# First-layer weight rows loaded by groups of 32 partitions, and two small products moved ahead of the router's product

## The reference

```python
nx = layer_norm(x) * gamma + beta
q, k, v = nx @ Wq, ctx @ Wk, ctx @ Wv
weights = softmax(q k^T / 16)                    # over the 64 prototypes
evidence = weights @ v
combined = concat([nx, evidence, anchor])        # anchor: one row of 256 per batch
probs = softmax(combined @ router_W + router_b)  # 3 experts
h = silu(combined @ e_w1[e] + e_b1[e])           # 768 -> 512, per expert
routed = sum_e probs[e] * (h @ e_w2[e] + e_b2[e])
g = sigmoid(silu(combined @ gate_w1 + gate_b1) @ gate_w2 + gate_b2)
out = x + g * (routed @ out_w + out_b)
```

## Time and profile before

| what | value |
|---|---|
| median of 3 runs | 459.05 us (458.45 to 460.62) |
| the profiled execution | 458.27 us, span of its instructions 456.5 us |
| PE busy | 444.9 us (97%), 2070 matmuls |
| DVE / ACT / POOL busy | 269.5 (59%) / 246.4 (54%) / 93.8 us (21%) |
| mean granted PE clock | 0.987 |
| DMA queue of SP | 48.33 MB |
| the chain that ended last | PE 87%, DVE 3%, DMA 3%, ACT 3%, issue 2% |

### The profile page before, as it was taken

The page is one execution under the profiler, slowest core; times in us unless marked ns, Lnnn a source line. Parts: engine busy times, 40 slices in busy tenths (PEclk is TensorE's granted clock), DMA queues, the critical chain, the costliest instruction groups (busy, mean ns, idle before and its releaser), DMA issues.

```text
span 456.5 us, 6005 instructions
## 1 busy us (share of the span) xinstructions
PE 444.9 (97%) x2070; PEld 363.2 (80%) x2070; DVE 269.5 (59%) x535; ACT 246.4 (54%) x389; POOL 93.8 (21%) x82
## 2 busy tenths in 40 slices
PE   7989999999999999999999999999999999999993
PEld 6677877888888888878888888878888888888882
DVE  3665356588566765575556856565564845544356
ACT  2355554666846556645755465555646484545431
POOL 1200003050212420350232320351133122222200
PEclk9988999999999999999999999999999999999997
DMA  7586733832446336362346316542443425224202
GB/s 231 184 223 172 198 102 65 189 93 47 128 105 156 83 85 132 100 140 90 72 86 169 71 69 139 125 106 94 93 93 93 96 72 110 48 47 114 48 0 46
DMA packets 72911, 49.26 MB, mean 108 GB/s; under 512 B 49226, under 2 KB 62322, under 8 KB 72882
## 3 DMA queue, kind: packets, MB, share of 16 engines
q1 hardware_dynamic: 71552, 48.33, 43.0%
q10 hardware_dynamic: 1218, 0.29, 0.3%
q0 software_dynamic: 112, 0.26, 0.2%
HBM read 26.77 MB, written 7.39 MB: 75 GB/s over the span
## 4 chain that ended last, share of the span: by engine, by line
PE 87%; DVE 3%; DMA 3%; ACT 3%; issue 2%; ACTq 1%; SPq 0%; DVEq 0%
PE bank L555 34%; PE bank L825 30%; PE bank L801 10%; DMA vw<-vw_pair 3%; PE bank L583 2%; PE bank L695 2%; PE bank L620 2%; PE bank L653 2%; PE bank L665 1%; PE bank L585 1%; ACT hf L998 1%; DVE work L1255 1%; ACT h L1001 1%; DVE xn L1042 1%; ACTq L358 1%
## 5 line engine op out<-in xcount | busy, mean ns | idle before, releaser
L1311 DVE TENSOR_TENSOR h<-hf,h 128x512 fp32r<-128x512 f32 x112 | 99.8, 891 | 151.8 <-ACT h L1001 150.6
L555 PE MATMUL bank<-nx,w1n 128*128 128x512 f32 x672 | 175.8, 397 | 0.0
L825 PE MATMUL bank<-h,w 128*128 128x512 f32 x576 | 148.1, 392 | 0.2
L998 ACT ACTIVATE hf<-bank,zb 128x512 f32<-128x512 f32 x112 | 77.2, 689 | 131.3 <-PE bank L801 130.1
L555 PEld LDWEIGHTS bank<-nx,w1n 128*128 128x128 f32 x672 | 123.9, 188 | 25.7 <-issue 0.5
L825 PEld LDWEIGHTS bank<-h,w 128*128 128x128 f32 x576 | 107.9, 188 | 25.5 <-DVE work L1255 1.0
L1001 ACT ACTIVATE h<-bank,zb 128x512 fp32r<-128x512 f32 x112 | 76.4, 682 | 0.0
L801 PE MATMUL bank<-wT,vw 128*128 128x512 f32 x224 | 70.4, 395 | 0.5 <-DMA vw<-vw_pair 0.5
L801 PEld LDWEIGHTS bank<-wT,vw 128*128 128x128 f32 x224 | 42.1, 189 | 10.0 <-DMA vw<-vw_pair 1.0
L1350 POOL TENSOR_TENSOR xq<-xq,quad 128x512 f32<-128x512 f32 x14 | 18.2, 1323 | 100.9 <-DVE quad L1070 100.9
L1343 POOL TENSOR_TENSOR rstd<-ve,minus_half 128x4 f32<-128x4 f32 x8 | 10.1, 1259 | 127.3 <-DVE ve L1031 127.3
(11 more groups left out here) (139 smaller groups left out, 414.4 us busy)
## 6 DMA issues: line engine op xcount, KB each, us to landing
vw<-vw_pair SPq DMA_DIRECT2D x48, 256.0 KB, 3.7
xn<-in_x_dram SPq DMA_DIRECT2D x8, 512.0 KB, 4.2
p_bc<-prob_dram SPq DMA_DIRECT2D x8, 512.0 KB, 4.5
xq<-in_x_dram SPq DMA_DIRECT2D x32, 128.0 KB, 2.8
out_dram<-xq SPq DMA_DIRECT2D x28, 128.0 KB, 3.1
stage<-in_L_xcond_e_w_dram SPq DMA_DIRECT2D x6, 512.0 KB, 5.5
xhat_dram<-xn SPq DMA_DIRECT2D x6, 512.0 KB, 2.9
quad<-xhat_dram SPq DMA_DIRECT2D x24, 128.0 KB, 2.8
```

The costliest lines, as they stand in the source:

```text
L555: mm = pe.matmul(dst, lhs(a), rhs(c), start=first and i == 0, stop=last and i == n - 1)
L825: mm = pe.matmul(o, lhs, h[:, s % HRING, a, :], start=c == 0 and i == 0, stop=c == COUNT[g] - 1 and i == 2)
L998: act.activation(hf[:, s % 2, :], z, ACT.Silu, bias=zb[:, j, b:b + 1]).then_inc(s_h, 1)
L1311: dve.tensor_tensor(h[:, s % HRING, LO, :], hf[:, s % 2, :], h[:, s % HRING, HI, :].bitcast(F32), ALU.subtract).then_inc(s_hlo, 1)
```

## The change

Two edits. The first: the x part of a group's first layer was loaded in two DMAs, one per half `k` of the features, each of 128 partitions (in memory `q k a`: 4 groups `q` of 32 rows `a`). Now it is loaded in four DMAs, one per group `q`, each of 32 partitions with both halves `k`. Bytes, source rows and destination are the same. The second: `anchor_product(1)` and `b2_product` leave their place ahead of unit 1 and stand ahead of `logits(0)` on PE, `z_bias(1)` and `b2_out` ahead of `router_max(0)` on DVE.

```diff
-            transfers = sum(KC if k == "n" else 1 for k, _ in staged[u % STAGES:u + 1:STAGES])
+            transfers = sum(QUADS if k == "n" else 1 for k, _ in staged[u % STAGES:u + 1:STAGES])
...
-        FIRST_PLAN = {1: ["bias", "zb1"], 2: ["vwp2", "ewT0", "split2"], ...
+        FIRST_PLAN = {2: ["vwp2", "ewT0", "split2"], ...
...
-                    rows_k = first_layer(g, 0).rearrange("(q k a) n -> k q a n", k=KC, a=QROWS)
-                    for k in range(KC):
-                        sp.dma_start(stage[:, u % STAGES, k, 0:COUNT[g] * PART], rows_k[k])\
+                    rows_q = first_layer(g, 0).rearrange("(q k a) n -> q a k n", k=KC, a=QROWS)
+                    for q in range(QUADS):
+                        sp.dma_start(stage[q * QROWS:(q + 1) * QROWS, u % STAGES, :, 0:COUNT[g] * PART], rows_q[q])\
                           .then_inc(s_stage[u % STAGES], 16)
...
             first_layer_nx(1)
+            anchor_product(1)
+            b2_product()
             logits(0)
...
             w1_lo(1)
+            z_bias(1)
+            b2_out()
             router_max(0)
```

More of the change, by code:

```diff
@@ L254, in stage_of @@
             u = staged.index((kind, g))
-            transfers = sum(KC if k == "n" else 1 for k, _ in staged[u % STAGES:u + 1:STAGES])
+            transfers = sum(QUADS if k == "n" else 1 for k, _ in staged[u % STAGES:u + 1:STAGES])
             return u % STAGES, (s_stage[u % STAGES], 16 * transfers)
-        FIRST_PLAN = {1: ["bias", "zb1"], 2: ["vwp2", "ewT0", "split2"], 3: ["fold0"], 4: ["zb2"], 5: ["ewT1"],
+        FIRST_PLAN = {2: ["vwp2", "ewT0", "split2"], 3: ["fold0"], 4: ["zb2"], 5: ["ewT1"],
                       6: ["xT", "split3"], 7: ["fold1"], 8: ["vwp3", "zb3", "vsplit1"], 9: ["ewT2", "vsplit2"], 10: ["sc"],
@@ L286, in plan @@
                     "zb": ((n,), {"dve": ["z_bias"]}, {}),
-                    "bias": ((), {"dve": ["b2_out"]}, {}),
                     "split": ((n,), {}, {"act": ["w1_hi"], "dve": ["w1_lo"]}),
@@ L680, in _ @@
             steps = {"xT": x_transpose, "sc": scores, "wt": w_transpose, "lg": logits, "vwp": pair_product,
-                     "ewT": w2_transpose, "fold": w2_fold, "zb": anchor_product, "bias": b2_product}
+                     "ewT": w2_transpose, "fold": w2_fold, "zb": anchor_product}
             done = 0
@@ L1183, in v_lo @@
                 dve.tensor_tensor(lo, src, hi.bitcast(F32), ALU.subtract).then_inc(s_vlo, 1)
-            steps = {"v_lo": v_lo, "b2_out": b2_out, "stats": stats_of, "normalise": normalise, "nx_full": nx_full, "x_turn": x_turn, "y_turn": y_turn,
+            steps = {"v_lo": v_lo, "stats": stats_of, "normalise": normalise, "nx_full": nx_full, "x_turn": x_turn, "y_turn": y_turn,
                      "nx_lo": nx_lo,
```

## The result

In the first comparison the changed kernel takes 453.7 us in the median of 7 runs (452.74 to 456.46), the kernel before 458.69 (7 runs); the ratio is 0.9898, 95% interval 0.9864 to 0.9932. The forecast was 455.5 with a range of 453.6 to 458.0. The measured time lies at the very end of that range, 0.1 us inside, nearer to the first rival (the clock doesn't fall, 453.8) than to the forecast.

What follows compares the result with a forecast made beforehand. PE was taken as the bound, busy 444.9 of 456.5 us, losing time only to two holes and a slow clock. Gains of 1.16 + 0.69 + 1.73 = 3.6 us from the median 459.05 gave 455.5, range 453.6 to 458.0.

Steps and rivals of the forecast that it cites:

- first rival: Slow stretch after 28.5 us: the clock does not fall at all, gain 5.25 us, 453.8 us; chance 0.13.
- The hole: PE idle from 28.51 to 29.67 ahead of the router's product; the two moved products fill it, gaining 1.16 us.
- Four engines and queues: Old x-part loads run on four DMA engines, delaying transfers queued behind; new loads use 16, so `vw` lands sooner.
- The wait of unit 6: PE waits in unit 6 for `vw` of group 2; the new loads remove it, gaining 0.69 us.
- loads don't spread: Rival: new loads run no faster than 98 GB/s, `vw` of group 2 still waits; 456.2 us, chance 0.10.
- The clock: PE's slow-clock stretch within 28.5 to 41.5 us, costing 3.4 us; 1.73 us of it gained, bounds 0 to 3.4.
- The forecast case: Clock falls at 31.4 as before, after the anchor product, so only the later part is paid; 455.5 us, chance 0.46.
- the dear clock: Rival: the slow clock costs as much as before, gain 1.85 us, 457.2 us; chance 0.26.
- No slower side: Slower rival: 32-partition loads at half rate or less delay `w1_hi(1)` and the router's product; 461.5 us or more, chance 0.05.

Runs made afterwards that it cites:

- filled hole: Kernel before, with six dense matmuls of 256 columns on zeros added ahead of the router's product, their result unused; 459.73 us, ratio 1.0012.

## Why the prediction was right, and where not

**The hole: right.** 1.16 us, and the products fill it: the router's product starts within 0.1 us of the forecast, and `b2_product` does not wait for POOL's copy.

**Four engines and queues: right,** and now tested, not only read from a share: 2 and 4 as the outermost dimension gave 45 and 98 GB/s, and with 32 the limit was gone (242 GB/s, other loads included).

**The wait of unit 6: right in the profile, wrong as a price.** The step took 0.69 us for the loads, as if the two edits could be summed. With the order alone the wait is 2.1 us, group 2's narrow load holds ACT and with it SP's issue, and PE's lead is lost. In medians: order alone 459.4, loads alone 457.6, both 453.7, before 459.6. The loads are worth 2.1 us by themselves and 5.7 on top of the order. The prediction moved PE forward by 1.16 + 1.73 = 2.9 us in one term and left it where it was in the other. By its own rows the old copy lands at 48.9 + 12.7 = 61.6, and a PE that is 2.9 us earlier needs it at 58.1: a wait of 3.5 us and not 0.69. So the rival "loads don't spread", priced at 456.2, should have been priced at no gain; the order alone, which has the old loads everywhere, took 459.4. It also looked for the victims of the old load only at the copy of `vw`. It did not ask when the x part of group 2 lands and who reads it: `w1_hi(2)` got it at 42.86 with a faster PE, 2.8 us after ACT was free, and that keeps SP's issue of the copy where it was.

**The clock: the term that was mis-sized.** Forecast a gain of 1.73 us, in the profile 3.4. It falls in about half of the runs (9 of 19 lie below 0.995) and then costs about 1.8 or 3.6 us, by the middles of the heaps (452.8, 454.7, 456.5). The forecast case, a fall that costs half of before, is the middle heap, with 6 of 19 runs, and its profile fits the forecast closely: second layer of unit 0 at 38.42, forecast 38 to 39. The likeliest is the first heap, which the prediction had at 0.13; the dear clock, which it had at 0.26, is the third, with 3 of 19. So the times of all three cases were seen, and it was their chances that were off. That the median fell inside the range is partly luck: nine of nineteen runs are below it, and the later comparisons gave 453.9 and 453.59. That the length of the row of small products decides is supported from both sides: lengthened, the clock was below 0.992 in ten of ten runs; broken in two, it was never below 0.994 in twelve.

**No slower side.** Four loads cost 1.92 us to issue at 43.09, against 1.15 for two and the 2.3 to 3.4 feared (2.88 against 2.09 for group 2's at 28.98). SP's copy follows early enough.

**Open.** Loads alone gain 2.1 us in the median while the two profiles differ by 0.9. A larger wait of unit 6 in other runs of the kernel before would explain it (it was 1.6 us in the profile with the filled hole, which has the old loads), and the 69 runs of before do spread over 5.9 us, against 2.7 us for the twelve with the new loads; but no profile of such a run of before was taken. Nor is it shown why the clock falls in one run and not in the next.

## What to carry to other kernels

Look at the DMA share: here a stretch that held at 0.26 or 0.13 while work was queued was a load on four or two engines, and its victims were the transfers queued behind it; a dimension of 32 outermost on both sides cured it. When a step on the bound engine is moved forward, ask which transfer was just in time for the next one, and price its wait with the lead, not without it: the lead is kept only if the loads can follow. And count rows of small products as a danger to the clock: 3 us of them in one piece brought it down in 9 of 19 runs here, the same work in two pieces in none of twelve.

## What the runs showed of the hardware

The clock fell while PE was busy without a gap: 13.00 of 13.00 us busy and a mean clock of 0.87 or 0.74, with a row of matmuls of 8 and 3 columns ahead of the fall or around it. A wait of PE can cost more than its length: behind the waits of 2.10 us (order alone) and 2.22 us (only group 2's loads new) the clock fell and cost another 1.7 us, so that such a hole cost nearly twice what the wait list shows; behind the one of 1.64 us (filled hole) it did not fall. And a copy of 64 partitions that stands behind a load on four engines took 12.7 us to land, though with loads on all engines, more of them issued ahead, it took 5.0.
